# Second norm's rows turned by way of DRAM and VectorE, and the shared expert's gate and up weights held in TensorE while pairs of token tiles move

## The chip, the cores and the metric

The kernel runs on one core of a Trainium2 chip. The metric is device microseconds of that core for one execution, taken as the median of several executions.

## What is computed

1024 tokens (16 sequences of 64) of width 512 in float32 pass four residual blocks. The reference, cut to what matters here:

```
x = x + linear_attention(norm(x), ctx, ctx)
x = x + ffn(norm(x))                            # low rank, 1376 wide, gate and up with silu
x = x + cross_attention(norm(x), ctx)           # 16 heads of 96, 4 key/value heads; "second norm" here
x = x + moe(norm(x))                            # 16 experts, top 4, plus a shared expert

# cross attention: queries of the latents; keys and values of [context, latents]
hidden = concatenate([ctx, latents], axis=1)
q = latents @ Wq.T;  k = hidden @ Wk.T;  v = hidden @ Wv.T

# shared expert, 256 wide
out = out + silu(x @ Sg.T) * (x @ Su.T) @ Sd.T
```

The norms are numbered 1 (before the ffn), 2 (before the cross attention, the "second norm" of the title) and 3 (before the experts).

## The kernel before

Tokens are cut into J = 8 tiles of 128 rows; the width of 512 is KC = 4 chunks of 128. Every engine walks one hand-written list, `prog`, of steps such as ("ln_z", 2, j), and does its own part of each step in that order; semaphores tie the engines together. So the order of `prog` is the order in every engine's queue, and an instruction that waits holds up all behind it on its engine. SyncE (SP in the profile) has a straight list of transfers of its own, in which a wait holds up all later transfers too.

A matrix product wants the normalized rows turned, with the width on the partitions: the buffer zT. A norm of tile j is three steps. "ln_stat": VectorE takes mean and variance, GpSimd the root. "ln_z": VectorE writes the normalized rows to one of two row buffers, zrow (line 964). "ln_t": TensorE turns four blocks of 128x128 into a PSUM bank (line 1150, `transposes`), and ScalarE copies the bank to zT (line 631).

The places that the change touches, in order of time:

- The ffn runs over two halves of the tokens (h = 0, 1), each with NF = 11 slices c of the inner width. A step of the loop is f_gu(h, c), a gate and an up product of 512 columns (lines 1253 and 1254), a silu on ScalarE (689), a multiplication on VectorE (973), and f_z(h, c - 1), a product with the multiplied slice before (1263). The second norm of tiles 0 to 3 stands inside the loop of h = 1. Behind it are f_out of tiles 4 to 7 (TensorE line 1273, VectorE's addition line 979).
- Then come the queries of tiles 0 and 1, q(0, 0) to q(0, 3), and between them the key and value products of tiles 0 to 3; the second norm of tiles 4 to 7 stands there. VectorE and ScalarE copy each q out of PSUM (lines 986 and 699). The first scores, s(0), follow, and right behind them the first key product over tiles 4 to 7.
- The cross attention goes over 32 half sequences. Between its last steps stand the first sh_gu, the shared expert's gate and up products.
- In the tail, after the attention, stand the rest of the shared expert, the third norm of tile 7, its routing ("gate", "gate_v", "place", "count", "route") and "tables", a small product whose result tells every engine which rows and experts come when. Only then can SyncE load the first block of rows of the expert loop (line 411, four transfers of 64 KB that gather 32x128 pieces), VectorE turn it (line 891, 32x32 blocks) and TensorE begin with 36 blocks of the experts.

Shared expert, per tile j: sh_gu(j) multiplies the tile (stationary) with gate and up weights together (512 columns moving, four products); silu and multiplication give 256 columns zs, with the tokens on the partitions; sh_t(j) turns them on TensorE (two blocks), ScalarE copies them to zgT (line 753), and sh_d(j) multiplies with the down weights. The first four sh_gu are put aside (graw) and get their silu in the tail.

```
dense(ps[:, 4 + j % 2, :], lambda k: zT[:, k, j * P:(j + 1) * P],
      lambda k: wsh[:, k * D:(k + 1) * D], KC)
```

Of the kernel before, what the change touches and what calls it, by code (L numbers as in the profile page):

```python
# [12 lines left out]
P = 128  # L13
# [23 lines left out]
def build(nc, x_d, ctx_d, ctxT_d, cst_d, u1_d, v1_d, u2_d, v2_d, b1_d, b2_d,  # L37
# [3 lines left out]
    quads_d = slot_d.rearrange("(c a j) (b e) -> c b j a e", a=4, j=QD, b=4)  # L41

    id_d = nc.dram_tensor("slots", (P, 2 * P), F32, kind="Internal").ap()

    with ExitStack() as stack:
# [59 lines left out]
        zs = r1[:, 3072:3072 + J * I].rearrange("p (j i) -> p j i", j=J)  # L105
# [9 lines left out]
        kvm = sb("kvm", [P, 2, P])  # L115
        gw = sb("gw", [P, KC, E])
# [83 lines left out]
        s_z = sem("z_done")  # L200
        s_xb = sem("x1_plus_b2_done")
# [41 lines left out]
        s_ht = sem("shared_act_transposed")  # L243
        s_htc = sem("shared_act_copied")
# [80 lines left out]
        prog.append(("q", 0, 0))  # L325
        for i, u in enumerate(lat_units[0]):
# [5 lines left out]
            if 1 <= i < 5:  # L332
                prog.append(("ln_t", 2, 3 + i))
# [20 lines left out]
        for n in range(NU + 1):  # L354
# [22 lines left out]
            if n == 13:  # L377
# [3 lines left out]
        prog += [("sh_silu", j) for j in range(EARLY)]  # L381
        prog += [("op1", J - 1), ("ln_stat", 3, J - 1), ("place", J - 2), ("sh_t", 0), ("sh_gu", 4), ("ln_z", 3, J - 1),
                 ("sh_d", 0), ("ln_t", 3, J - 1), ("sh_t", 1), ("sh_d", 1), ("gate", J - 1), ("gate_v", J - 1), ("sh_gu", 5),
                 ("sh_t", 2), ("place", J - 1), ("count",), ("route", 0), ("sh_gu", 6), ("route", 1), ("sh_t", 3),
                 ("sh_d", 2), ("sh_d", 3), ("sh_gu", 7), ("tables",), ("sh_t", 4), ("sh_t", 5), ("sh_d", 4),
                 ("sh_t", 6), ("sh_d", 5), ("sh_t", 7), ("sh_d", 6), ("sh_d", 7)]

        def order(kinds):
            return {step: i for i, step in enumerate(p for p in prog if p[0] in kinds)}
# [26 lines left out]
        def kv_bank(n):  # L416

            return ps[:, 6 + n % 2 if n < EARLY_KV else 7, :]

# [5 lines left out]
        def _(sp):  # L425
# [40 lines left out]

            sp.wait_ge(s_fo, J)
# [3 lines left out]
            sp.dma_start(wv2, wv_d.rearrange("p (k m) -> p k m", k=KC)).then_inc(s_wkv2, 16)  # L471
            load_wo(0)
# [145 lines left out]
        def _(act):  # L618
# [15 lines left out]
            for step in prog:  # L634
# [109 lines left out]
                elif kind == "sh_silu":  # L744
                    j = step[1]
                    act.wait_ge(s_hraw, j + 1)
                    if j >= 2:
                        act.wait_ge(s_hz, j - 1)
# [379 lines left out]
        def _(pe):  # L1128
# [24 lines left out]
            def normed(layer, j):  # L1153

                pe.wait_ge(s_trc, TRN[("ln_t", layer, j)] + 1)
# [409 lines left out]
```

## Time and profile before

| | us |
|---|---|
| median of 3 runs | 711.25 |
| lowest and highest | 709.66, 711.31 |
| the profiled execution | 708.29 |
| its span, first to last instruction | 706.5 |
| TensorE busy | 682.1 (97%) |
| VectorE busy | 341.8 (48%) |
| ScalarE busy | 200.9 (28%) |
| mean granted TensorE clock | 0.994 |

The span is the stretch in which the profile sees instructions; the profiled execution's time holds 1.8 us more around it. Busy TensorE time is the union of its products' durations, of which each overlaps the next. In all rows a 32-bit product has two records, so that "x8" is four products; a turned block has one.

### The profile page before, as it was taken

The numbers are of one execution on the slowest core, as the hardware profiler recorded it, in microseconds if no ns is written. First come the engines' busy times: TensorE is split into PE (matmuls) and PEld (weight loads), VectorE is DVE, ScalarE is ACT, GpSimd is POOL, SyncE is SP. The second block draws the span as 40 slices with busy tenths as digits, with TensorE's granted clock in tenths as the row PEclk, the third lists the DMA queues.
The fourth block names the chain that finished last, engine by engine and source line by source line (L and its number), as shares of the span: only waits on it lengthen the run. The fifth ranks groups of instructions, "written<-read, shape, count | busy, mean of one in ns | idle before, by whom it ended". The sixth has DMA issues, their size and how long they took to land.

```text
span 706.5 us, 9696 instructions
## 1 busy us (share of the span) xinstructions
PE 682.1 (97%) x2444; PEld 394.6 (56%) x2445; DVE 341.8 (48%) x834; ACT 200.9 (28%) x563; POOL 176.2 (25%) x226
## 2 busy tenths in 40 slices
PE   9999899999999999999999999999999999999992
PEld 6555343446777777777776666554444444444440
DVE  4997433433224545686666667456233333333331
ACT  5453332313345433323333333231111111111110
POOL 2354210101000000004505233346023433333342
PEclk9999999999999999999999999999999999999997
DMA  9999997003000020001104003513866757768444
GB/s 341 409 421 420 422 420 320 1 29 150 1 1 0 1 90 0 1 1 61 60 1 150 30 31 111 189 60 92 274 164 111 179 103 186 183 131 234 92 73 60
DMA packets 54642, 98.99 MB, mean 140 GB/s; under 512 B 6560, under 2 KB 27808, under 8 KB 53952
## 3 DMA queue, kind: packets, MB, share of 16 engines
q1 hardware_dynamic: 24848, 69.41, 26.2%
q0 software_dynamic: 8816, 18.00, 12.7%
q10 hardware_dynamic: 20944, 11.15, 5.4%
q8 instruction: 18, 0.29, 0.2%
q14 instruction: 16, 0.13, 0.1%
HBM read 44.50 MB, written 54.17 MB: 140 GB/s over the span
## 4 chain that ended last, share of the span: by engine, by line
PE 81%; DMA 6%; DVE 5%; issue 2%; ACT 1%; POOL 1%; ACTq 1%; POOLq 1%; SPq 0%; DVEq 0%
PE ps L1159 46%; PE ps L1335 12%; DMA out<-rq,sidx 5%; PE ps L1304 4%; PE ps L1150 4%; PE ps L1320 4%; PE ps L1253 3%; PE ps L1254 3%; PE ps L1263 3%; DVE rq L941 2%; PE ps L1273 1%; DMA xr<-in_x 1%; DMA rq<-slot_rows 1%; DVE st L909 1%; ACTq L411 1%
## 5 line engine op out<-in xcount | busy, mean ns | idle before, releaser
L1159 PE MATMUL ps<-kv,rq 128*128 x432 | 192.4, 594 | 1.1 <-DVE rq L891 0.6
L1159 PEld LDWEIGHTS ps<-kv,rq 128*128 128x128 f32 x432 | 78.8, 190 | 88.3 <-issue 87.7
L1159 PE MATMUL ps<-zT,r 128*128 128x256 f32 (+1 forms) x424 | 103.4, 400 | 0.9 <-ACT kv L670 0.9
L1159 PEld LDWEIGHTS ps<-zT,r 128*128 128x128 f32 x424 | 79.4, 190 | 20.3 <-issue 10.2
L1335 PE MATMUL ps<-r 128*128 128x512 f32 x192 | 85.1, 593 | 0.0
L598 POOL DMA_INDIRECT out<-rq,sidx x36 | 56.7, 1574 | 110.7 <-DMA out<-rq,sidx 82.7
L525 POOL TENSOR_SCALAR ve<-mv 128x1 f32<-128x1 f32 x32 | 7.1, 223 | 292.4 <-DVE mv L910 292.4
L708 ACT ACTIVATE r<-ps,snm 128x128 f32<-128x128 f32 x128 | 45.3, 366 | 82.7 <-DVE snm L997 82.7
L1089 DVE TENSOR_TENSOR rq<-ps,rq 128x256 f32<-128x256 f32 x36 | 15.3, 424 | 97.3 <-ACT rq L764 97.3
L1335 PEld LDWEIGHTS ps<-r 128*128 128x128 f32 x192 | 35.2, 190 | 38.3 <-issue 38.3
L764 ACT ACTIVATE rq<-ps 128x256 f32<-128x256 f32 x36 | 13.8, 384 | 119.6 <-PE ps L1159 108.2
L986 DVE COPY rq<-ps 32x256 f32<-32x256 f32 x48 | 20.5, 427 | 50.8 <-PE ps L1159 50.3
L1100 DVE TENSOR_SCALAR rq<-ps,wts 128x512 f32<-128x512 f32 x36 | 27.0, 751 | 31.2 <-issue 13.3
L564 POOL DMA_INDIRECT slot_rows<-zrow,sloti x32 | 33.4, 1045 | 34.5 <-DVE sloti L1067 26.3
L1159 PE MATMUL ps<-r,zT 128*128 128x512 f32 (+1 forms) x96 | 39.9, 558 | 0.0
L1159 PE MATMUL ps<-r,rq 128*128 128x512 f32 x80 | 36.5, 595 | 1.0 <-ACT rq L753 1.0
L631 ACT COPY r<-ps 128x512 f32<-128x512 f32 x40 | 23.4, 586 | 45.8 <-PE ps L1150 45.7
L973 DVE SCALAR_TENSOR_TENSOR rq<-ps,r,rq 128x512 f32<-128x512 f32 (+1 forms) x22 | 16.4, 750 | 41.3 <-ACT rq L689 41.3
L1304 PE MATMUL ps<-kv,rq 96*128 96x128 f32 x256 | 34.8, 279 | 0.0
L1320 PE MATMUL ps<-r,kv 128*96 128x256 f32 x128 | 32.9, 379 | 1.3 <-DVE r L1013 1.3
L532 POOL DMA_INDIRECT slots<-tokw,sloti x32 | 31.2, 976 | 9.5 <-issue 9.5
L1304 PEld LDWEIGHTS ps<-kv,rq 96*128 96x128 f32 x256 | 32.6, 192 | 1.4
(176 smaller groups left out, 871.0 us busy)
## 6 DMA issues: line engine op xcount, KB each, us to landing
slot_rows<-rq SPq DMA_DIRECT2D x4, 8192.0 KB, 50.7
kv<-in_experts SPq DMA_DIRECT2D x54, 256.0 KB, 4.3
rq<-slot_rows ACTq DMA_DIRECT2D x136, 64.0 KB, 3.4
r<-in_Wq SPq DMA_DIRECT2D x1, 3072.0 KB, 21.3
r<-in_Wo SPq DMA_DIRECT2D x2, 1536.0 KB, 7.9
r<-in_ctx SPq DMA_DIRECT2D x8, 256.0 KB, 8.3
xr<-in_x SPq DMA_DIRECT2D x8, 256.0 KB, 8.4
out<-xr SPq DMA_DIRECT2D x8, 256.0 KB, 3.9
```

What stands on the lines that cost most here:

```text
L532: pool.indirect_dma_start(out=id_d.rearrange("a (b c) -> (a b) c", c=2), out_offset=bass.IndirectOffsetOnAxis(ap=sloti[:, j, k:k + 1], axi ...
L564: pool.indirect_dma_start(out=slot_d, out_offset=bass.IndirectOffsetOnAxis(ap=sloti[:, j, k:k + 1], axis=0), in_=zrow[:, LNN[("ln_z", 3, j ...
L598: pool.indirect_dma_start(out=out_d, in_=ylast[:, par, :] if last else yrow[:, par, :], in_offset=None, out_offset=bass.IndirectOffsetOnAx ...
L631: act.copy(dst, ps[:, n % 2, :] if len(dst.shape) == 2 else ps[:, n % 2, :].rearrange("p (k t) -> p k t", k=KC)).then_inc(s_trc, 1)
L708: e = act.activation(prob[:, n % 2, u, :], ps[:, 2 + n % 2, u * P:(u + 1) * P], ACT.Exp, bias=snm[:, n % 4, u:u + 1], scale=SCALE, accum_o ...
L1100: dve.tensor_scalar(ylast[:, par, :] if last else yrow[:, par, :], ps[:, 6 + par, :], wts[:, bass.ds(col, 1)], None, ALU.mult).then_inc(s_ ...
L1150: mm = pe.transpose(bank[:, c * P:(c + 1) * P], src[:, c * P:(c + 1) * P], ident)
L1159: mm = pe.matmul(out, lhs(k), rhs(k), start=(k == 0), stop=(k == n - 1))
L1253: pe.matmul(ps[0:m, 2 + n % 2, :], v1[:, c * P:c * P + m], pT, start=True, stop=True)
L1304: mm = pe.matmul(ps[:, 2 + n % 2, u * P:(u + 1) * P], qT[0:HD, q % 2, b % 4, h0:h0 + 2, :].rearrange("p h s -> p (h s)"), kT[0:HD, g, b, : ...
L1320: mm = pe.matmul(ps[0:HD, 6, 256 * g:256 * g + 256], v[:, b, c0:c0 + HD], probT[:, n % 2, 256 * g:256 * g + 256], start=True, stop=True)
L1335: mm = pe.matmul(ps[:, 7, :], oT[:, j % 2, m, :], wo[:, m, :], start=(m == 0), stop=(m == NQT - 1))
```

## The change

Two edits.

**The second norm's turning.** TensorE and ScalarE have no part in ("ln_t", 2, j) any more. SyncE stores the tile's 128x512 normalized rows to DRAM (256 KB), waits for that, and loads them again into a buffer zquad with four transfers of 64 KB, each of which gathers pieces of 128 floats for 32 partitions. VectorE turns zquad in blocks of 32x32 into zT. What lands in zT has the width in another order over partitions and chunks, and so have the weights Wq, Wk, Wv and the turned context, which the host lays out in that order; ScalarE writes the exponentials of the context in it as well. There is one zquad: the loads of tile j wait until tile j - 1 is turned. The steps of tiles 0 to 2 stand after slices 6, 8 and 10 of the ffn's second half, that of tile 3 behind its last f_out, those of tiles 4 to 7 one step later than before.

**The shared expert.** A sh_gu(i) now takes a pair of tiles: an even i gives the gates of pair i // 2, an odd one the ups. Blocks of 128 columns of the weights are stationary and 256 tokens move, eight products of 256 columns. The result has the inner width on the partitions, so sh_t, its turned blocks and ScalarE's copies, goes away; silu and multiplication are done once for a pair, over 512 columns.

```
     zrow_d = nc.dram_tensor("second_norm_rows", (2, P, D), F32, kind="Internal").ap()
     zquad_d = zrow_d.rearrange("n (a j) (b e) -> n b j a e", a=4, b=4)
...
-                if c % 2 == 0 and 1 <= i <= len(beside):
+                if h == 0 and c % 2 == 0 and 1 <= i <= len(beside):
                     prog.append(("ln_t", *beside[i - 1]))
+                if h == 1 and c in (6, 8, 10):
+                    prog.append(("ln_t", 2, c // 2 - 3))
...
-        prog.append(("q", 0, 0))
+        prog += [("ln_t", 2, 3), ("q", 0, 0)]
...
-            if 1 <= i < 5:
-                prog.append(("ln_t", 2, 3 + i))
+            if 2 <= i < 6:
+                prog.append(("ln_t", 2, 2 + i))
...
-        prog += [("sh_silu", j) for j in range(EARLY)]
-        prog += [("op1", J - 1), ("ln_stat", 3, J - 1), ("place", J - 2), ("sh_t", 0), ("sh_gu", 4), ("ln_z", 3, J - 1),
-                 ("sh_d", 0), ("ln_t", 3, J - 1), ("sh_t", 1), ("sh_d", 1), ("gate", J - 1), ("gate_v", J - 1), ("sh_gu", 5),
-                 ("sh_t", 2), ("place", J - 1), ("count",), ("route", 0), ("sh_gu", 6), ("route", 1), ("sh_t", 3),
-                 ("sh_d", 2), ("sh_d", 3), ("sh_gu", 7), ("tables",), ("sh_t", 4), ("sh_t", 5), ("sh_d", 4),
-                 ("sh_t", 6), ("sh_d", 5), ("sh_t", 7), ("sh_d", 6), ("sh_d", 7)]
+        prog += [("sh_silu", a) for a in range(EARLY // 2)]
+        prog += [("op1", J - 1), ("ln_stat", 3, J - 1), ("place", J - 2), ("sh_gu", 4), ("ln_z", 3, J - 1), ("sh_d", 0),
+                 ("ln_t", 3, J - 1), ("sh_d", 1), ("gate", J - 1), ("gate_v", J - 1), ("sh_gu", 5), ("place", J - 1),
+                 ("count",), ("route", 0), ("sh_gu", 6), ("route", 1), ("sh_d", 2), ("sh_d", 3), ("sh_gu", 7), ("tables",),
+                 ("sh_d", 4), ("sh_d", 5), ("sh_d", 6), ("sh_d", 7)]
...
+            def turn_rows(j):
+
+                sp.wait_ge(s_z, LNN[("ln_z", 2, j)] + 1)
+                sp.dma_start(zrow_d[j % 2], zrow[:, LNN[("ln_z", 2, j)] % 2, :]).then_inc(s_zst[j % 2], 16)
+                if j:
+                    sp.wait_ge(s_zt2, j)
+                sp.wait_ge(s_zst[j % 2], 16 * (j // 2 + 1))
+                for b in range(4):
+                    sp.dma_start(zquad[b * QD:(b + 1) * QD, :].rearrange("p (a e) -> p a e", a=4),
+                                 zquad_d[j % 2, b, :, :, :]).then_inc(s_zld, 16)
+
+            for j in range(4):
+                turn_rows(j)
             sp.wait_ge(s_fo, J)
             sp.wait_ge(s_xb, J)
             sp.wait_ge(s_act, 2 * NF)
             sp.dma_start(wk2, wk_d.rearrange("p (k m) -> p k m", k=KC)).then_inc(s_wkv2, 16)
             sp.dma_start(wv2, wv_d.rearrange("p (k m) -> p k m", k=KC)).then_inc(s_wkv2, 16)
+            for j in range(4, J):
+                turn_rows(j)
             load_wo(0)
...
+                        if old[1] == 2:
+                            dve.wait_ge(s_zst[old[2] % 2], 16 * (old[2] // 2 + 1))
...
+                elif kind == "ln_t" and step[1] == 2:
+                    j = step[2]
+                    dve.wait_ge(s_zld, 64 * (j + 1))
+                    dve.wait_ge(s_pt, j // 4 + 1)
+                    dve.transpose(zT[:, :, j * P:(j + 1) * P].rearrange("p k (a j) -> p a k j", a=4),
+                                  zquad[:, :].rearrange("p (a k i) -> p a k i", a=4, k=KC)).then_inc(s_zt2, 1)
...
                 elif kind == "sh_silu":
-                    j = step[1]
-                    act.wait_ge(s_hraw, j + 1)
-                    if j >= 2:
-                        act.wait_ge(s_hz, j - 1)
-                    act.activation(sg[:, j % 2, :], graw[:, j, 0:I], ACT.Silu).then_inc(s_hsil, 1)
-                elif kind == "sh_t":
-                    j = step[1]
-                    act.wait_ge(s_ht, j + 1)
-                    act.copy(zgT[:, j % 2, :], ps[:, 2 + j % 2, 0:I]).then_inc(s_htc, 1)
+                    a = step[1]
+                    act.wait_ge(s_hraw, 2 * a + 1)
+                    act.activation(shg[a], graw[:, 2 * a, :], ACT.Silu).then_inc(s_hsil, 1)
...
                 elif kind == "sh_gu":
-                    normed(3, j)
-                    dense(ps[:, 4 + j % 2, :], lambda k: zT[:, k, j * P:(j + 1) * P],
-                          lambda k: wsh[:, k * D:(k + 1) * D], KC).then_inc(s_hg, 1)
-                elif kind == "sh_t":
-                    transposes(ps[:, 2 + j % 2, :], zs[:, j, :], I // P).then_inc(s_ht, 1)
+                    normed(3, 2 * a)
+                    normed(3, 2 * a + 1)
+                    for c in range(2):
+                        at = (2 * hf + c) * P
+                        mm = dense(shared_bank(i)[:, c * 2 * P:(c + 1) * 2 * P], lambda k: wsh[:, k * D + at:k * D + at + P],
+                                   lambda k: zT[:, k, 2 * a * P:2 * (a + 1) * P], KC)
+                    mm.then_inc(s_hg, 1)
```

What it moves on VectorE, in the ffn's second half from its slice 6 to the first q: the rows "rq<-ps,r,rq" are the slices' multiplications, "zrow" the normalized rows, "xr<-ps,xr" the additions of f_out, "rq<-ps 32x4x64" the first q's copies. Before:

```order
L973 SCALAR_TENSOR_TENSOR rq<-ps,r,rq 128x512
L909 BN_STATS st<-xr 128x6
L910 BN_AGGR mv<-st 128x2
L973 SCALAR_TENSOR_TENSOR rq<-ps,r,rq 128x512
L964 TENSOR_SCALAR zrow<-xr,mv,rstd 128x512
L973 SCALAR_TENSOR_TENSOR rq<-ps,r,rq 128x512 x2
L973 SCALAR_TENSOR_TENSOR rq<-ps,r,rq 96x512
L979 TENSOR_TENSOR xr<-ps,xr 128x512 x4
L986 COPY rq<-ps 32x4x64 x3
```

The same place of the changed kernel, on VectorE, where lines 1005, 990, 1011 and 1018 are the former 973, 964, 979 and 986:

```order
L1005 SCALAR_TENSOR_TENSOR rq<-ps,r,rq 128x512
L932 BN_STATS st<-xr 128x6
L933 BN_AGGR mv<-st 128x2
L996 STREAM_TRANSPOSE zT<-zquad 128x4x4x32
L1005 SCALAR_TENSOR_TENSOR rq<-ps,r,rq 128x512
L990 TENSOR_SCALAR zrow<-xr,mv,rstd 128x512
L1005 SCALAR_TENSOR_TENSOR rq<-ps,r,rq 128x512
L996 STREAM_TRANSPOSE zT<-zquad 128x4x4x32
L1005 SCALAR_TENSOR_TENSOR rq<-ps,r,rq 128x512
L1005 SCALAR_TENSOR_TENSOR rq<-ps,r,rq 96x512
L996 STREAM_TRANSPOSE zT<-zquad 128x4x4x32
L1011 TENSOR_TENSOR xr<-ps,xr 128x512 x4
```

Four turnings have come in there (the fourth is the row behind the last one shown), each of which waits for its loads and stands ahead of a multiplication or an addition.

TensorE in the tail, from sh_t(0) to "count" before; "ps<-cst,r" are the blocks of sh_t, "r,zT" is sh_gu, "r,rq" sh_d, "cst,zrow" the third norm of tile 7, "gw,zT" its gate:

```order
L1150 MATMUL ps<-cst,r 128x128 x2
L1159 MATMUL ps<-r,zT 128x512 x4
L1159 MATMUL ps<-r,rq 128x512 x2
L1150 MATMUL ps<-cst,zrow 128x128 x4
L1150 MATMUL ps<-cst,r 128x128 x2
L1159 MATMUL ps<-r,rq 128x512 x2
L1159 MATMUL ps<-gw,zT 128x16 x4
L1159 MATMUL ps<-r,zT 128x512 x4
L1150 MATMUL ps<-cst,r 128x128 x2
L1352 MATMUL ps<-mask,cst 128x16
L1353 MATMUL ps<-mcum,cst 128x16
L1361 MATMUL ps<-mcum,cst 128x16
```

TensorE at the same place of the changed kernel; sh_d is now "ps<-r" and sh_gu "zT,r":

```order
L1196 MATMUL ps<-zT,r 128x256 x8
L1196 MATMUL ps<-r 128x512 x2
L1184 MATMUL ps<-cst,zrow 128x128 x4
L1196 MATMUL ps<-r 128x512 x2
L1196 MATMUL ps<-gw,zT 128x16 x4
L1196 MATMUL ps<-zT,r 128x256 x8
L1394 MATMUL ps<-mask,cst 128x16
L1395 MATMUL ps<-mcum,cst 128x16
L1403 MATMUL ps<-mcum,cst 128x16
```

The turned blocks are gone, and each sh_gu has become eight products of 256 columns instead of four of 512.

## Rows read from the trace of the kernel before

**Rows 1.** The page's first part: busy time, share of the span, instructions.
```profile
PE 682.1 (97%) x2444; PEld 394.6 (56%) x2445; DVE 341.8 (48%) x834; ACT 200.9 (28%) x563; POOL 176.2 (25%) x226
```

**Rows 2.** Timeline of TensorE, 143 to 200 us: start, duration, what, [idle before].
```profile
143.81 0.60 PE L1150 MATMUL ps<-cst,zrow 128*128 128x128 f32 x4
144.25 1.02 PE L1253 MATMUL ps<-rq,r 128*128 128x512 f32 x2
...
145.97 1.02 PE L1263 MATMUL ps<-rq,r 128*128 128x512 f32 x2
146.83 1.02 PE L1253 MATMUL ps<-rq,r 128*96 128x512 f32 x2
...
152.12 4.03 PE L1273 MATMUL ps<-r,rq 128*128 128x512 f32 x8 [0.68 <-ACT rq L693]
155.99 5.34 PE L1159 MATMUL ps<-zT,r 128*128 128x256 f32 x24
161.17 7.03 PE L1159 MATMUL ps<-zT,rq 128*128 128x512 f32 x16
168.03 0.60 PE L1150 MATMUL ps<-cst,zrow 128*128 128x128 f32 x4
...
199.09 1.06 PE L1304 MATMUL ps<-kv,rq 96*128 96x128 f32 x8
```

**Rows 3.** Timeline of VectorE, 124 to 166 us.
```profile
125.00 0.54 DVE L964 TENSOR_SCALAR zrow<-xr,mv,rstd 128x512 f32<-128x512 f32 x1
...
143.94 0.75 DVE L973 SCALAR_TENSOR_TENSOR rq<-ps,r,rq 128x512 f32<-128x512 f32 x1 [1.37 <-ACT rq L689]
...
153.36 0.69 DVE L979 TENSOR_TENSOR xr<-ps,xr 128x512 f32<-128x512 f32 x1 [3.09 <-PE ps L1273]
...
165.04 0.55 DVE L964 TENSOR_SCALAR zrow<-xr,mv,rstd 128x512 f32<-128x512 f32 x1 [1.42 <-POOL rstd L526]
```

**Rows 4.** VectorE's 32x32 turning, line 891: durations in ns, first and last start.
```profile
L891 DVE STREAM_TRANSPOSE rq<-rq x36: 699/701/712, 495.4 to 680.3; 128x512 f32<-128x512 f32 x36
```

**Rows 5.** Line 411's 64 KB loads: SyncE's eight in the timeline, and all 144.
```profile
488.38 4.41 SPq L411 DMA_DIRECT2D rq<-slot_rows  x8
...
DMA to landing us min/median/max: 1.8/3.4/7.7
```

**Rows 6.** Line 497's eight stores of 256 KB, each a tile's rows to DRAM.
```profile
DMA to landing us min/median/max: 2.9/3.9/4.3
```

**Rows 7.** Stretches: busy PE, PEld, DVE, ACT, POOL; clock; DMA share; GB/s.
```profile
127.00:150.00 23.00, 22.57 (x65) 10.43 (x63) 10.19 (x18) 7.97 (x13) 2.37 (x6) 1.00 0.00 1
488.00:497.00 9.00, 8.26 (x22) 3.75 (x23) 2.70 (x5) 1.13 (x4) 3.69 (x4) 1.00 0.56 157
```

**Rows 8.** Timeline of TensorE in the tail, 462 to 497 us.
```profile
462.47 0.42 PE L1150 MATMUL ps<-cst,r 128*128 128x128 f32 x2
462.73 3.60 PE L1159 MATMUL ps<-r,zT 128*128 128x512 f32 x8
...
468.32 0.38 PE L1150 MATMUL ps<-cst,r 128*128 128x128 f32 x2
469.43 1.98 PE L1159 MATMUL ps<-r,rq 128*128 128x512 f32 x4 [0.73 <-ACT rq L753]
...
476.16 0.38 PE L1361 MATMUL ps<-mcum,cst 128*128 128x16 f32 x2
...
487.08 0.25 PE L1386 MATMUL ps<-cst,cols 128*6 128x48 f32 x2
...
496.32 4.12 PE L1159 MATMUL ps<-kv,rq 128*128 x9 [0.58 <-DVE rq L891]
```

**Rows 9.** Timeline of VectorE in the tail: a shared multiplication, the routing's last row.
```profile
480.52 0.42 DVE L1077 TENSOR_TENSOR r<-ps,rq 128x256 f32<-128x256 f32 x1 [0.19 <-ACT rq L743]
...
485.71 0.17 DVE L838 TENSOR_REDUCE cols<-r 128x1 f32<-128x16 f32 x1
```

**Rows 10.** Chain of waits, the longest piece between "tables" and the expert loop.
```profile
489.91 5.42 DMA rq<-slot_rows
```

More of the change, by code:

```diff
@@ L115, in build @@
         kvm = sb("kvm", [P, 2, P])
+        zquad = sb("zquad", [P, D])
         gw = sb("gw", [P, KC, E])
@@ L200, in build @@
         s_z = sem("z_done")
+        s_zst = [sem(f"second_norm_stored{i}") for i in range(2)]
+        s_zld = sem("second_norm_loaded")
+        s_zt2 = sem("second_norm_transposed")
         s_xb = sem("x1_plus_b2_done")
@@ L656, in _ @@
                     copied(step, ekT[:, j % 2, :])
-                elif kind == "ln_t":
+                elif kind == "ln_t" and step[1] != 2:
                     copied(step, zT[:, :, step[2] * P:(step[2] + 1) * P])
@@ L959, in _ @@
                         old = [p for p in prog if p[0] == "ln_z"][n - 2]
-                        dve.wait_ge(s_tr, TRN[("ln_t", *old[1:])] + 1)
+                        if old[1] == 2:
+                            dve.wait_ge(s_zst[old[2] % 2], 16 * (old[2] // 2 + 1))
+                        else:
+                            dve.wait_ge(s_tr, TRN[("ln_t", *old[1:])] + 1)
                         if old[1] == 3:
@@ L1070, in _ @@
                 elif kind == "sh_silu":
-                    j = step[1]
-                    dve.wait_ge(s_hsil, j + 1)
-                    dve.tensor_tensor(zs[:, j, :], graw[:, j, I:2 * I], sg[:, j % 2, :], ALU.mult).then_inc(s_hz, 1)
-                elif kind == "sh_gu" and step[1] >= EARLY:
-                    j = step[1]
-                    dve.wait_ge(s_hsil, j + 1)
-                    dve.tensor_tensor(zs[:, j, :], ps[:, 4 + j % 2, I:2 * I], sg[:, j % 2, :],
-                                      ALU.mult).then_inc(s_hz, 1)
+                    a = step[1]
+                    dve.wait_ge(s_hsil, a + 1)
+                    dve.wait_ge(s_hraw, 2 * a + 2)
+                    dve.tensor_tensor(zs[:, a, :], graw[:, 2 * a + 1, :], shg[a], ALU.mult).then_inc(s_hz, 1)
+                elif kind == "sh_gu" and step[1] >= EARLY and step[1] % 2:
+                    i = step[1]
+                    a = i // 2
+                    dve.wait_ge(s_hsil, a + 1)
+                    dve.wait_ge(s_hg, i + 1)
+                    dve.tensor_tensor(zs[:, a, :], shared_bank(i), shg[a % 2], ALU.mult).then_inc(s_hz, 1)
                 elif kind == "sh_d":
@@ L1153, in normed @@
             def normed(layer, j):
-                pe.wait_ge(s_trc, TRN[("ln_t", layer, j)] + 1)
+                if layer == 2:
+                    pe.wait_ge(s_zt2, j + 1)
+                else:
+                    pe.wait_ge(s_trc, TRN[("ln_t", layer, j)] + 1)
             def dense(out, lhs, rhs, n):
@@ L1160, in dense, with shared_act @@
                 return mm
+            def shared_act(j, c):
+                at = (2 * c + j % 2) * P
+                return zs[:, j // 2, at:at + P]
             def half_unit(j, i):
@@ L1227, in _ @@
                               lambda k: weights[1][:, k, :], KC).then_inc(s_pr, 1)
-                elif kind == "ln_t":
+                elif kind == "ln_t" and step[1] != 2:
                     n = LNN[("ln_z", *step[1:])]
@@ L1388, in _ @@
                     j = step[1]
-                    pe.wait_ge(s_htc, j + 1)
+                    pe.wait_ge(s_hz, j // 2 + 1)
                     if j == 0:
```

60 lines of the change are left out of this document (31 added, 29 removed).

## The prediction

> **What bounds the kernel now.** I read the page first: TensorE is busy for 97% of the span [rows 1], so time on TensorE is the currency, and a change pays what it takes off TensorE, less what it makes TensorE wait. Then I read TensorE's timeline at the places of the two edits. Around the second norm, from 127 to 200 us, the reader is to see starts that follow each other without a gap: a slice of the ffn takes 146.83 - 144.25 = 2.58 us, and only around f_out is there a wait, 0.68 us [rows 2]. The tail is TensorE without idle time but for 0.73 us ahead of sh_d(1), up to "tables" at 487.08; behind it, the loop starts at 496.32, and what ends the wait for it is not the work that TensorE does in between but a transfer of the first rows, 5.42 us from issue to landing, and its turning [rows 8, 10].
>
> **First edit, what it takes off TensorE.** The four turned blocks of a tile start at 143.81, the next product at 144.25: 0.44 us a tile, eight tiles, **3.5 us** [rows 2]. All eight lie in the stretch without gaps. ScalarE's copies go too, and nobody waited for them. In the slices of the ffn that have no turned blocks beside them TensorE also runs at 2.58 us without a gap, so the loop is not held by silu and multiplication once the blocks are gone.
>
> **What it adds.** On VectorE a turning of 128x512, 0.70 us as in line 891 [rows 4]. On SyncE per tile a store of 256 KB, for which the nearest rows give 2.9 to 4.3 us to landing, median 3.9 [rows 6], and four loads of 64 KB, issued 4.41 / 8 = 0.55 us apart, each 1.8 to 7.7 us to landing, median 3.4 [rows 5]. I call the landing of a load L. Those rows come from stretches in which the DMA engines are busy for some 56% of the time; where tiles 0 to 3 are turned they are idle (share 0.00) [rows 7]. So I expect L near 1.8, take 3.4 as the careful value, and keep 7.7 as the far end.
>
> Whether this shows is a question of dates. I write what stands in the trace of before, less 0.44 us for each group of blocks already gone, and the store as 3.9.
>
> - Tile 0: its rows are ready at 125.5 [rows 3], loaded long before slice 6 is multiplied at 137.5 (slice 8's multiplication is at 143.94 before [rows 3], two slices and one group later than slice 6's, and two groups are gone by then). The turning waits in the queue behind that multiplication and the statistics of tile 3 (some 0.9 us) and ends at 139.8.
> - Tile 1: its loads wait for that; the last of four is issued at 141.55, and the turning ends at 141.55 + L + 0.7 = 145.7 with L = 3.4. The multiplication of slice 9, due at 145.2, moves back by 0.5 us. It has room: slice 8's ends at 144.69 and f_z wants it at 145.97 [rows 2, 3], 1.28 us later.
> - Tile 2: SyncE stores it once the loads of tile 1 are issued (142.1), the store lands at 146.0, the last load is issued at 147.7, the turning ends at 148.4 + L = 151.8. Behind it in the queue is the addition of f_out(4), due at 153.36 - 1.74 = 151.62 [rows 3], for which f_out(6) waits on TensorE: 0.2 us late at L = 3.4, nothing below 3.2.
> - Tile 3: stored at 148.3, landed 152.2, loads to 153.9, turned at 154.6 + L = 158.0. The key product that needs it is due at 161.17 - 1.74 = 159.43 [rows 2]; 1.4 us to spare. q(0, 0) needs only tiles 0 and 1.
> - Tiles 4 to 7: tile 4's rows are ready at 165.59 - 1.74 = 163.85 [rows 3]. A tile then takes store and four issues, 3.9 + 2.3 = 6.2 us, since the next store goes while the loads land. Tile 7 is stored at 182.5 and turned at 182.5 + 3.9 + 1.65 + L + 0.7 = 192.2. The product that needs it follows s(0), at 199.09 - 3.49 + 0.9 = 196.5 [rows 2]: 4.3 us to spare. VectorE's copies of q stand behind these turnings; q(0, 2) is the tight one: tile 6 is turned at 192.2 - 6.2 = 186.0, and q(0, 3), which wants the bank, starts 5.2 us ahead of s(0), at 190.4.
>
> Behind SyncE's waits stand Wk, Wv and Wo: Wk and Wv are issued at the old date, Wo once tile 7's loads are issued, before s(0), and its first use is well behind s(0). The first edit is thus worth 3.5 us, with 0 to 0.2 us back; I take 0. The ordered exponentials and the host's layouts change no count of bytes or columns; I cost them at nothing.
>
> The Trainium skill speaks against the edit: its page "VectorE: DVE Perf Modes", section "Rules for kernel authors", says to turn 128x128 on TensorE where PSUM will do as the destination, and on VectorE only blocks of 32. Turning by turning the rows agree (0.44 us on TensorE, 0.70 on VectorE, and a round trip besides). By that rule alone the edit loses; it is decided by who is idle, and that is the first rival below. "DMA: Bandwidth & Descriptors", section "Anatomy of one DMA", has some 2.0 us fixed plus bytes at 436 GB/s; by that, called an estimate, a load takes 2.2 us and a store 2.6, and no date above is missed.
>
> **Second edit.** Products: four of 512 columns cost (168.03 - 161.17) / 8 = 0.858 us each, eight of 256 cost (161.17 - 155.99) / 12 = 0.432 [rows 2], so a sh_gu costs 3.45 instead of 3.43, **0.2 us more** over eight. Taken away before "tables" are sh_t(0), 462.73 - 462.47 = 0.26; sh_t(1) with the wait behind it, 469.43 - 468.32 = 1.11 [rows 8]; sh_t(2) and sh_t(3), 0.22 each: **1.8 us**. sh_t(4) to (7) stand after "tables", where TensorE waits for rows anyway; they are worth nothing, and TensorE's idle time ahead of the loop grows from 0.58 to about 2 us. The multiplication and ScalarE's silu of a pair are wider but half as many; sh_d(0) finds zs(0) ready long before.
>
> Is "tables" still TensorE's to give? The routing on VectorE starts with "count" (476.16) and ends at 485.88, 9.7 us; TensorE comes to "tables" 10.9 us after "count" [rows 8, 9]. Afterwards 10.7 against some 9.3, since the 0.42 us multiplication inside the routing goes. TensorE stays later by 1.4 us. From "tables" on everything is a fixed lag (9.24 us to 496.32), so the loop starts 1.6 us plus 3.5 us earlier, and the loop itself is unchanged.
>
> **Sum.** 3.5 + 1.8 - 0.2 = 5.1 us off the profiled execution's 708.29, 703.2. The median of the runs shown is 2.96 us above that execution; the same 5.1 off 711.25 gives **706.1**.
>
> **Rivals.**
> 1. *The round trip is seen, and the kernel gets slower.* If loads land as slowly as the slowest of before, one buffer zquad makes a chain. Bound by landings, tile 1 ends at 142.25 + L, tile 2 at 144.7 + 2L, tile 3 at 147.15 + 3L against 159.43: a loss of 3L - 12.3, from L = 4.1. In the second four the loss is 4L - 19.1, from L = 4.8. Together 7L - 31.3: that eats the 5.1 us at L = 5.2 and is 2.1 us slower than before from L = 5.5; at 7.7 it is 22.6 lost, a time of 728.8. For it: a load of this very shape took 5.42 us at 489.91. Against it: there the engines were busy for 56%, here for nothing. Chance 0.05. A partial form, L from 3.6 to 4.8, costs 0.5 to 3 us and gives 706.6 to 709; 0.10.
> 2. *The tail gives nothing.* The landing of the first rows is set by other traffic (GpSimd's scatters), not by "tables"; then a start of 1.6 us less is eaten and 3.5 us remain: 707.8. For it: 5.42 against a median of 3.4. Against it: those scatters come from the same chain, which moves as well. 0.12.
> 3. *The change does less than it says*, because VectorE's queue holds back the multiplications of the ffn or the copies of q by more than their room: 1 to 3 us lost somewhere, 707 to 709; in 0.08 I put all such. Anything that gives more than 5.5 us, such as shorter waits at the loop's start, 0.05.
>
> **Chances.** The forecast holds with 0.60 and has 705.3 to 707. A change of under 0.3% (2.1 us) cannot be told from none here. Faster by more: all of the forecast, the second rival, and most of the others, 0.87; within: 0.07; slower: 0.06. For eight in ten I go from 703.5 (the runs' own spread and some more gain) to 709.
>
> **What would show it.** Right: no rows "ps<-cst,zrow" between 127 and 185, slices of 2.58 us, q(0, 0) at about 154.2, s(0) at 195.6, "tables" at 482.0, the loop at 491.2. Right for the round trip: landings below 3 us and VectorE's turnings with no waits by TensorE behind them. Wrong: an idle gap of TensorE at f_out(6), ahead of the first key product or behind s(0), released by a turning; or "tables" early while the first transfer's landing grows by as much. A clock below 1.00 after the 2 us gap ahead of the loop would also break the sum.

## The result

The changed kernel took 708.55 us (median of 20 runs, 707.03 to 713.04), the kernel before 711.7 us on the same chip (20 runs, 709.66 to 714.65): a ratio of 0.996, 95% interval 0.9947 to 0.9974. It is faster by 3.15 us; 5.1 were forecast. Executions of one kernel spread over some 5 us on this chip, so the medians of 20 are compared. The profiled execution of the changed kernel took 709.7 us, with a span of 707.6 and a mean granted clock of 0.987.

The page's first part, answering to [rows 1]:

```profile
PE 679.5 (96%) x2460; PEld 404.0 (57%) x2461; DVE 346.2 (49%) x838; ACT 193.3 (27%) x543; POOL 176.3 (25%) x226
```

TensorE's timeline at the first edit, answering to [rows 2]:

```profile
149.19 1.12 PE L1305 MATMUL ps<-rq,r 96*128 96x512 f32 x2 [0.76 <-DVE rq L1005]
150.99 4.03 PE L1315 MATMUL ps<-r,rq 128*128 128x512 f32 x8 [0.68 <-ACT rq L720]
154.85 5.34 PE L1196 MATMUL ps<-zT,r 128*128 128x256 f32 x24
160.03 10.46 PE L1196 MATMUL ps<-zT,rq 128*128 128x512 f32 x24
...
196.19 1.06 PE L1346 MATMUL ps<-kv,rq 96*128 96x128 f32 x8
```

The turned blocks are gone, TensorE waits for no turning, and s(0) starts 2.90 us earlier, though this execution's first transposition came 0.77 us later (9.27 against 8.50). The new transfers in the page's part on DMA issues (count, KB each, median us to landing):

```profile
second_norm_rows<-zrow SPq DMA_DIRECT2D x8, 256.0 KB, 2.2
```

And the four loads a tile, from the view of the buffer zquad (least, median and most of their time to landing):

```profile
DMA to landing us min/median/max: 1.8/1.9/2.3
```

The tail of TensorE, answering to [rows 8]:

```profile
482.80 0.25 PE L1425 MATMUL ps<-cst,cols 128*6 128x48 f32 x2 [0.21 <-issue]
483.50 7.10 PE L1196 MATMUL ps<-r 128*128 128x512 f32 x16 [0.44 <-issue]
496.01 10.08 PE L1196 MATMUL ps<-kv,rq 128*128 x16 [5.41 <-SPq L520]
```

"tables" is 4.28 us earlier than before, but the loop starts only 0.31 us earlier: 13.21 us lie between them instead of 9.24, TensorE is idle for 5.41 of these, and the loop's first row (sixteen records, eight products) then takes 10.08 us (7.13 in an execution without this, below). The 0.21 us ahead of "tables" is a wait for the routing, whose last row on VectorE ends at 482.75 here. What the other engines did behind "tables", from the timelines of ScalarE, VectorE and SyncE:

```profile
486.11 0.19 ACT L779 CAST tab<-ps 6x48 int32<-6x48 f32 x1 [9.77 <-remote]
...
482.67 1.28 DVE L1119 TENSOR_TENSOR xr<-ps,xr 128x512 f32<-128x512 f32 x2
484.06 0.69 DVE L1112 TENSOR_TENSOR r<-ps,rq 128x512 f32<-128x512 f32 x1
492.44 1.29 DVE L1119 TENSOR_TENSOR xr<-ps,xr 128x512 f32<-128x512 f32 x2 [7.68 <-remote]
...
488.87 6.89 SPq L418 DMA_DIRECT2D rq<-slot_rows  x8
```

ScalarE takes the tables' product 3.3 us after it started, where 0.3 to 0.4 is usual. VectorE adds sh_d(4) at 492.44, though the product was done before 486. SyncE issues the first load 6.07 us after "tables" (1.30 before) and needs 6.89 us for the eight (4.41 before, [rows 5]). This slowness of all three is called the lateness below. The stretches of the windows view (answering to [rows 7]; the number behind POOL's is the granted clock) show no traffic to blame, with a DMA share of 0.30 where before had 0.56, and the clock:

```profile
488.00:497.00 9.00, 3.59 (x8) 1.31 (x7) 2.58 (x4) 0.00 (x0) 2.52 (x3) 0.90 0.30 73
497.00:515.00 18.00, 18.00 (x44) 8.12 (x43) 4.64 (x8) 2.48 (x8) 0.18 (x1) 0.86 0.79 263
```

The two mean clocks together stand for (0.10 x 9 + 0.14 x 18) / 0.5 = 6.8 us at 1.2 GHz, at the end of the idle time and behind it.

The lateness is not only behind "tables". A shared multiplication on VectorE, some 9 us ahead of "tables", comes 2.04 us later than in the undisturbed execution of the same program (the second row, from the first group below), and the whole routing with it:

```profile
473.75 0.69 DVE L1112 TENSOR_TENSOR r<-ps,rq 128x512 f32<-128x512 f32 x1 [2.59 <-remote]
```

```profile
471.71 0.69 DVE L1112 TENSOR_TENSOR r<-ps,rq 128x512 f32<-128x512 f32 x1 [0.55 <-PE ps L1196]
```

### The profile page after: what moved, and what is told of

Read it like the earlier page. It is cut to its first block, busy times and chain, and to the rows that moved or that the text cites. A ratio compares the mean times of both kernels' runs of the same rounds, so it can differ in the third digit from the quotient of the medians.

```text
span 707.6 us, 9751 instructions
## 1 busy us (share of the span) xinstructions
PE 679.5 (96%) x2460; PEld 404.0 (57%) x2461; DVE 346.2 (49%) x838; ACT 193.3 (27%) x543; POOL 176.3 (25%) x226
## 4 chain that ended last, share of the span: by engine, by line
PE 79%; issue 8%; DVE 4%; DMA 3%; SPq 2%; ACT 1%; POOL 1%; POOLq 0%; DVEq 0%; ACTq 0%
PE ps L1196 48%; PE ps L1377 9%; PE ps L1346 4%; PE ps L1184 4%; PE ps L1362 4%; PE ps L1295 3%; PE ps L1296 3%; PE ps L1305 3%; DVE rq L964 2%; DMA r<-in_ctx 2%; DMA out<-rq,sidx 1%; PE ps L1315 1%; SPq L412 1%; SPq L418 1%; PE ps L1237 1%
## 5 line engine op out<-in xcount | busy, mean ns | idle before, releaser
L1196 PE MATMUL ps<-kv,rq 128*128 x432 | 195.3, 601 | 6.0 <-SPq L520 5.4
L1196 PE MATMUL ps<-zT,r 128*128 128x256 f32 (+1 forms) x552 | 132.5, 395 | 0.9 <-ACT kv L697 0.9
L1196 PEld LDWEIGHTS ps<-zT,r 128*128 128x128 f32 x552 | 103.4, 190 | 24.5 <-issue 11.2
L964 DVE RECIPROCAL rq<-ps 128x512 f32<-128x512 f32 x8 | 26.8, 3354 | 5.5 <-PE ps L1238 5.5
L1043 DVE COPY r<-ps 96x192 f32<-96x192 f32 x64 | 19.8, 348 | 19.1 <-PE ps L1362 18.5
```

Of the source, the lines that this page charges most:

```text
L964: link(dve.reciprocal(srec, ps[:, 5, :]))
L1196: mm = pe.matmul(out, lhs(k), rhs(k), start=(k == 0), stop=(k == n - 1))
```

## The experiments

All kernels of one group ran on one chip, beside runs of the kernel before on that chip; the three groups were on three chips. The theory after the first result: the change gives what it should up to "tables"; what is lost is the lateness and the low clock behind it. The rival: the tail gives nothing by the way the change is built. "Late" and "undisturbed" are said of a kernel's one profiled execution; the median is of all its runs.

**First group** (before: 709.19 us, 17 runs).

*First edit alone*: norm 2's rows through DRAM, the shared expert as before.

> The first edit alone (second norm turned by way of DRAM and VectorE; shared expert as before). Theory A, the loss sits in the tail: in the changed kernel's profile the first edit already showed its whole 3.5 us (s(0) 2.9 us earlier with a start 0.6 us later), so alone it gives 3.5 us off, ratio about 0.995, TensorE's granted clock stays at 1.00 up to the end of the loop (mean 0.994), and the gap ahead of the expert loop stays below 1.5 us. Rival B, the first edit costs something elsewhere (extra waits in the loop, or the longer program): ratio 0.997 or more, mean clock below 0.992.

Measured: 704.25 us (6 runs), ratio 0.9931 (0.9916 to 0.9945), a gain of 4.9 us: theory A, with 1.4 us more than its 3.5. The profile is undisturbed.

*Second edit alone*: the pairs, with norm 2 turned on TensorE.

> The second edit alone (shared expert's pairs; second norm as before). Theory A, what the second edit saves before the tables it gives back at the start of the expert loop: TensorE now idles there for more than 2 us, its granted clock falls to 0.5 for some 7 us, and the first products of the loop take some 3 us more; ratio 1.000 to 1.002, mean clock 0.987 to 0.990. Rival B, the idle gap costs nothing and the edit gives its 1.6 us: ratio 0.998, mean clock 0.994.

Measured: 707.2 us, ratio 0.9964 (0.9947 to 0.9982), its 12 runs spread from 703.59 to 709.45: neither theory, 2.0 us faster than before. Its profile is that of the slowest run. Nothing is late up to the loop, but VectorE then waits 5.09 us for a transfer of rows, TensorE is idle for 3.02 us inside the loop's start, and half clock follows.

*The changed kernel with fillers* that nothing reads:

```
 last_down()
+for n in range(5):
+    pe.matmul(ps[:, 5, :], ident, wsh[:, 0:D], start=True, stop=True)
```

> The changed kernel with five products of 512 columns put behind sh_d(7), ahead of the first gate and up product of the loop; their result is overwritten and nobody reads it. Theory A: TensorE idles some 4.3 us less there, its clock stays at 1.00 and the loop's first 16 records take 7.1 us instead of 10.1; ratio to the kernel before 0.992 to 0.994, mean clock 0.994. Rival B, the lower clock is not due to the gap, or costs nothing: ratio 0.996 as for the changed kernel, or above it where the rows come before the five products are through.

Measured: 705.79 us (6 runs), ratio 0.9952 (0.9935 to 0.997). No lateness and no gap here, so it does not decide between the theories.

*The changed kernel itself again.*

> The changed kernel once more, to see on the same chip how far its tail repeats. Theory A: ratio 0.996, mean clock 0.987 to 0.990, TensorE idle for 2 us or more ahead of the loop and at clock 0.5 in its first products. Of the profiled execution's late rows (the tables copied 3.3 us after their product, SyncE's four loads issued 1.4 us apart in place of 0.5): if they are a property of the kernel they are there again, if they belong to that execution the gap is about 2 us.

Measured: 701.65 us (701.26 to 702.01, 4 runs), ratio 0.9892 (0.9873 to 0.9911). Here the lateness was absent. Its tail, TensorE and then SyncE:

```profile
482.51 0.25 PE L1425 MATMUL ps<-cst,cols 128*6 128x48 f32 x2
482.69 7.13 PE L1196 MATMUL ps<-r 128*128 128x512 f32 x16
490.34 7.13 PE L1196 MATMUL ps<-kv,rq 128*128 x16 [0.52 <-DVE rq L914]
...
483.73 4.43 SPq L418 DMA_DIRECT2D rq<-slot_rows  x8
```

The same program, with "tables" at the same place within 0.3 us, starts the loop 5.7 us earlier than in the first profile and is 6.9 us faster in the median, on a chip where before is 2.5 us faster. The fillers, useless where nothing is late, held the loop back to 493.53 and cost 4.1 us.

**Second group** (before: 711.14 us, 31 runs): is the lateness the rule, what does an idle gap cost, and how much room has the round trip?

*The changed kernel a third time.*

> The changed kernel itself once more, beside the others of this call. In its first 20 runs it took 708.55 us, in the first experiment's company 701.65 (before: 709.19), and the difference stands in the trace at the expert loop's start: engines that take 2 to 7 us longer to react, 5.41 us of idle TensorE, then half clock. Theory A (that lateness is not a part of the change, but comes with some loadings of a program): the loop starts at about 490.3 and the time is 701 to 702.5 where it is absent, 706 to 709 with a granted clock below 0.990 where it is there; nothing in between stands on the tables or the turned rows. Theory B (the change's own shorter tail makes the lateness, and the 701.65 was luck): 707 to 709 here again.

Measured: 709.57 us (708.51 to 711.19, 10 runs), ratio 0.9978 (0.996 to 0.9995). The time is above both theories' ranges by some 0.5 us and does not part them; the lateness is back, in the same shape:

```profile
483.99 0.25 PE L1425 MATMUL ps<-cst,cols 128*6 128x48 f32 x2 [0.20 <-issue]
484.68 7.11 PE L1196 MATMUL ps<-r 128*128 128x512 f32 x16 [0.44 <-DVE xr L1119]
496.86 9.99 PE L1196 MATMUL ps<-kv,rq 128*128 x16 [5.08 <-DVE rq L914]
...
487.91 8.54 SPq L418 DMA_DIRECT2D rq<-slot_rows  x8
```

*Two dummy loads ahead of the first rows*:

```
+for r in range(2):
+    sp.dma_start(zquad[0:QD, :]..., zquad_d[0, 0, :, :, :]).then_inc(s_ex, 16)
+    sp.wait_ge(s_ex, 16 * (r + 1))
 for i in range(2):
     block_of = sp.value_load(tab[0:1, i:i + 1], min_val=0, max_val=P)
```

> The changed kernel with two dummy loads of 64 KB, one after the other, in SyncE's queue ahead of the first rows' loads: some 4 to 6 us more of idle TensorE ahead of the loop, as in the changed kernel's first profile but made on purpose. Theory A (an idle gap of this length costs more than itself, since the clock falls to half behind it; in the first profile 6.8 us at half clock cost 3 us): the granted clock is 0.5 for some microseconds behind the gap, and the time is the gap plus about 3 us above the changed kernel of this call, 708 to 711. Theory B (the gap costs itself alone, and the half clock had another cause): clock 1.00 and 705.5 to 707.5.

Measured: 711.84 us (10 runs), ratio 1.0004 (0.9985 to 1.0022): 2.3 us over the changed kernel of this group. The gap is there, 7.60 us of idle TensorE ahead of a loop at 497.80, and half clock behind it. But the changed kernel already had 5.08 us of gap and half clock on this chip, so the two loads added 2.5 us of gap, and these cost 2.3 us: of the price of half clock this comparison says nothing.

*The same with seven fillers.*

> The same two dummy loads, with seven products of 128x512 that nothing reads behind the last product of the shared expert (some 6.2 us of TensorE in the gap). Theory A: the clock stays at 1.00 and it is about 3 us faster than the one without the fillers, though it does more. Theory B: no faster than that, and slower by up to 1 us where the fillers outlast the landing.

Measured: 711.38 us (10 runs), ratio 0.9991 (0.9975 to 1.0008). The loop's first products (timeline) and a stretch from there on (windows), of the kernel without fillers and then of the one with them:

```profile
497.80 8.80 PE L1201 MATMUL ps<-kv,rq 128*128 x16 [7.60 <-SPq L525]
```

```profile
498.00:515.00 17.00, 17.00 (x42) 7.78 (x43) 4.66 (x9) 2.48 (x8) 0.00 (x0) 0.91 0.87 285
```

```profile
493.07 6.17 PE L1484 MATMUL ps<-r,cst 128*128 128x512 f32 x14
501.13 7.13 PE L1201 MATMUL ps<-kv,rq 128*128 x16 [1.89 <-SPq L525]
```

```profile
501.00:515.00 14.00, 13.27 (x35) 6.22 (x36) 4.26 (x8) 1.68 (x5) 0.00 (x0) 1.00 0.87 284
```

That a long gap of TensorE is followed by half clock, and that products in the gap prevent it, is shown: theory A had the mechanism. Its price of 3 us is not borne out. The loop's first row took 1.7 us more (8.80 against 7.13), and yet from the loop's start to the end of the span both need the same (708.0 - 497.80 = 210.2; 711.2 - 501.13 = 210.1). The medians differ by 0.5 us, which these runs cannot tell from nothing, and not by 3. Over all fourteen profiles the same stretch takes 208.1 to 210.2 us where the loop starts at full clock and 210.2 to 214.0 us where half clock stands at its start (214.0 is the second edit alone in the first group, with its 3.02 us of gap inside the stretch). So any price from nothing to some 3 us fits, and it was not measured alone.

*Each tile's store three times in series* (round trip 4.4 us longer):

```
+for r in range(2):
+    sp.dma_start(zrow_d[j % 2], zrow[...]).then_inc(s_ex, 16)
+    sp.wait_ge(s_ex, 16 * (2 * j + r + 1))
 sp.dma_start(zrow_d[j % 2], zrow[...]).then_inc(s_zst[j % 2], 16)
```

> The changed kernel with every tile's store made three times, each waiting for the one before (a store lands in 2.2 us, so each round trip is 4.4 us longer). Theory A (the round trip is hidden by dates: tile 2's turning has 2 us of room ahead of the addition of f_out(4), tile 3's 3 us, tile 7's 9 us): by the dates of the profile tile 2 is now turned at 154.0 and holds f_out(6) back by about 1.8 us, tile 3 costs 0.5 more, tile 7 is turned at 200 where it is wanted at 197 to 199; 4 to 7 us slower than the changed kernel of this call. Theory B (the engines that wait for it have slack behind these dates): less than 2 us slower.

Measured: 712.8 us (10 runs), ratio 1.0024 (1.001 to 1.0039), 3.2 us over the changed kernel of this group. VectorE's turnings of tiles 2, 3 and 7, and TensorE where it waits:

```profile
151.09 0.71 DVE L1000 STREAM_TRANSPOSE zT<-zquad 128x512 f32<-128x512 f32 x1 [2.42 <-DMA zquad<-second_norm_rows]
159.71 0.71 DVE L1000 STREAM_TRANSPOSE zT<-zquad 128x512 f32<-128x512 f32 x1 [2.98 <-DMA zquad<-second_norm_rows]
...
199.41 0.71 DVE L1000 STREAM_TRANSPOSE zT<-zquad 128x512 f32<-128x512 f32 x1 [6.04 <-DMA zquad<-second_norm_rows]
```

```profile
193.47 5.42 PE L1200 MATMUL ps<-zT,r 128*128 128x256 f32 x24 [1.39 <-issue]
198.73 1.06 PE L1350 MATMUL ps<-kv,rq 96*128 96x128 f32 x8
200.38 8.85 PE L1200 MATMUL ps<-zT,r 128*128 128x512 f32 x32 [0.59 <-DVE zT L1000]
```

The first four tiles still hide all of it, since tile 2 is turned at 151.8 (154.0 by my dates, which put its store too late); the last ones show 1.39 + 0.59 = 2.0 us. (VectorE's copies of a q, at 192.11 behind tile 6's turning at 191.47, free the bank that the first of these waits for.) So a round trip 4.4 us longer a tile costs a few microseconds and no more: between the two theories.

**Third group** (before: 713.07 us, 21 runs): which edit brings the lateness?

*First edit alone, again.*

> The first edit alone once more, to see on a chip where the changed kernel's engines react late what each edit does there. Theory A (the lateness comes with the second edit's products, twice as many instructions on TensorE in the tail): tables to loop takes 8.5 to 9.2 us with ScalarE's CAST of the tables 0.4 us behind them, no half clock at the loop, 4 to 5 us faster than before (ratio about 0.994). Theory B (the lateness has nothing to do with either edit and comes with the chip): the CAST comes 1.5 to 3.5 us late here too and the ratio is above 0.996.

Measured: 706.97 us (706.2 to 707.37, 4 runs), ratio 0.9907 (0.9881 to 0.9933). TensorE, VectorE and SyncE in the tail:

```profile
484.01 0.25 PE L1423 MATMUL ps<-cst,cols 128*6 128x48 f32 x2
...
492.70 3.72 PE L1196 MATMUL ps<-r,rq 128*128 128x512 f32 x8 [2.75 <-ACT rq L778]
496.26 7.03 PE L1196 MATMUL ps<-kv,rq 128*128 x16
...
492.23 1.29 DVE L1119 TENSOR_TENSOR xr<-ps,xr 128x512 f32<-128x512 f32 x2 [7.27 <-remote]
...
486.55 8.14 SPq L420 DMA_DIRECT2D rq<-slot_rows  x8
```

Neither theory: the lateness is here too (VectorE 7.27 us, SyncE 8.14 for eight issues), but it sets in later, after the CAST, which comes 0.4 us behind "tables". TensorE's idle time comes in pieces between turned blocks, the longest 2.75 us, and its clock stays at 1.00.

*Second edit alone, again.*

> The second edit alone. Theory A: the late reactions are here (ScalarE's CAST 1.5 us or more behind tables, idle TensorE of 3 us or more at the loop's start, granted clock below 0.990) and eat the 1.6 to 3 us that it saves: ratio 0.998 to 1.003. Theory B: as in the first experiment's company, ratio 0.996.

Measured: 712.33 us (10 runs), ratio 0.9984 (0.9966 to 1.0002). "tables" at 486.28, the loop at 499.14 behind 5.06 us of idle TensorE, mean clock 0.986 to 0.990 over its runs: theory A.

*First edit, and the old gate and up products in halves*:

```
-dense(ps[:, 4 + j % 2, :], lambda k: zT[:, k, j * P:(j + 1) * P],
-      lambda k: wsh[:, k * D:(k + 1) * D], KC).then_inc(s_hg, 1)
+for hf in range(2):
+    mm = dense(ps[:, 4 + j % 2, hf * I:(hf + 1) * I], lambda k: zT[:, k, j * P:(j + 1) * P],
+               lambda k: wsh[:, k * D + hf * I:k * D + (hf + 1) * I], KC)
+mm.then_inc(s_hg, 1)
```

> The first edit alone, with each sh_gu(j) of the old shared expert done as eight products of 256 columns instead of four of 512: the second edit's count of TensorE instructions (64 instead of 32 a pair of tiles) without its pairs and without its order. Theory A (the instruction count makes the lateness): late reactions appear, TensorE idles ahead of the loop, 3 to 6 us slower than the first edit alone. Theory B (it is the order or the removed steps that matter): 0.2 us of product time more and no lateness, same as the first edit alone within 1 us.

Measured: 714.46 us (10 runs), ratio 1.0014 (0.9993 to 1.0034): 7.5 us slower than the first edit alone, for 0.2 us of product time, so theory A, by more than it said. TensorE and ScalarE in the timeline:

```profile
485.44 0.25 PE L1425 MATMUL ps<-cst,cols 128*6 128x48 f32 x2
485.62 0.66 PE L1184 MATMUL ps<-cst,r 128*128 128x128 f32 x4
494.25 3.78 PE L1196 MATMUL ps<-r,rq 128*128 128x512 f32 x4 [7.98 <-ACT rq L778]
...
504.09 7.03 PE L1196 MATMUL ps<-kv,rq 128*128 x16
...
488.89 0.38 ACT L768 ACTIVATE rq<-ps 128x256 f32<-128x256 f32 x1 [9.81 <-remote]
491.02 0.19 ACT L781 CAST tab<-ps 6x48 int32<-6x48 f32 x1 [1.75 <-remote]
```

No other kernel reacts so late: the silu of sh_gu(7) 3.4 us behind its product (485.4), the CAST 5.6 us behind "tables". The products are the same work on the same tiles; their number is doubled and their width halved, and with the number that of the loads of stationary blocks. Not all of the 7.5 us is lateness: the two profiles differ by 9.3 us, of which 6.4 lie between "tables" and loop (18.65 against 12.25) and 1.3 stand already at s(0), ahead of every product that the edit changes, where this execution had half clock at f_out (5.48 us for 4.03).

*The changed kernel with ScalarE kept busy*:

```
+elif kind == "sh_d" and step[1] < J - 1:
+    act.wait_ge(s_hd, step[1] + 1)
+    act.copy(spare[:, 16 * step[1]:16 * step[1] + 16], ident[:, 0:16])
```

> The changed kernel with seven tiny copies of 16 columns on ScalarE, one behind each product of sh_d, which nothing reads; ScalarE, idle for 9.8 us ahead of the tables' CAST in the changed kernel, then works at the same places as sh_t's copies did before. Theory C (an engine that has waited for long reacts late): the CAST comes 0.3 us behind tables, the loads are issued 2 to 3 us earlier, and it is 3 to 5 us faster than the changed kernel, ratio about 0.992. Theory A or B: the same as the changed kernel, 0.996 to 0.998.

Measured: 709.86 us (6 runs), ratio 0.9942 (0.9921 to 0.9964). The CAST still comes 2.6 us behind "tables" (485.16, 482.55), and "tables" to loop takes 12.95 us as in the kernel without the copies (12.87 in the second group). Theory C falls; that the ratio is nearer to 0.992 than to 0.998 is not explained by it, and the changed kernel itself did not run on this chip.

## Why the prediction was right, and where it was not

**First edit, 3.5 us: right.** Two profiles differ at s(0) by this edit alone and start alike (the first transposition at 9.24 and 9.27): the second edit alone has s(0) at 199.68, the changed kernel at 196.19, 3.49 us. Forecast dates of q(0, 0) and s(0) were 154.2 and 195.6, measured 154.85 and 196.19, both some 0.6 us later, in an execution whose start was 0.77 us late. L was 1.9 us, as hoped from the idle engines, and the store took 2.2 us, not the 3.9 that I wrote for it from [rows 6]; all dates of the chain had more room than I gave them. Rival 1 is excluded by landings of at most 2.3 us, and with trip times 4.4 us longer it would have cost 3.2 us. The Trainium skill's rule for VectorE ("VectorE: DVE Perf Modes", "Rules for kernel authors") is right turning by turning (0.70 us against 0.44) and did not decide, since TensorE was the engine without idle time. The Trainium skill's formula ("DMA: Bandwidth & Descriptors", "Anatomy of one DMA") gave an estimate of 2.2 and 2.6 us for load and store, and the trace has 1.9 and 2.2; the section fits it to DMAs that GpSimd issues, where SyncE issued these. By the medians the first edit alone gained more than 3.5 us, 4.9 and 6.1 on two chips. Of the surplus the undisturbed profile shows 0.75 us between "tables" and loop (8.49 against 9.24) and 1.3 behind it (208.8 against 210.2), which the prediction had put at nothing.

**Second edit ahead of "tables", 1.6 us: right where nothing is late.** From s(0) to "tables" it was 287.99 us before and is 286.33 in the changed kernel's undisturbed profile and in the second edit alone: 1.66. In the result's profile it is 286.61. The 1.4 us by which TensorE was to come later than the routing were gone there, since the routing had slipped by 2.04 us and ended 0.05 us ahead of "tables".

**"From tables on everything is a fixed lag (9.24 us)": this step failed**, and with it "the loop itself is unchanged" and TensorE's idle time of "about 2 us". The runs showed two lags in its place:

| profile | "tables" to loop, us | longest idle, us | half clock at the loop |
|---|---|---|---|
| before | 9.24 | 0.58 | no |
| changed, first group | 7.83 | 0.52 | no |
| first edit alone, first / third group | 8.49 / 12.25 | 0.24 / 2.75 | no / no |
| second edit alone, first / third group | 7.67 / 12.86 | 3.02 / 5.06 | yes / yes |
| changed, the result / second group | 13.21 / 12.87 | 5.41 / 5.08 | yes / yes |

(The 3.02 us lie inside the loop's start, behind its second block's products.) Without the lateness the tail gives more than forecast, because the first rows' transfers end earlier after "tables" (the last of the four took 4.08 us against 5.42 before): the lag shrinks by 1.4 us, the loop to the end by 0.9, and the changed kernel won 7.5 us. With it, the changed kernel loses 5.0 to 5.4 us between "tables" and loop (13.21 and 12.87 against 7.83), and in the result's profile 2.3 more behind it, where the low clock stands: from the loop's start to the span's end it is 211.6 us there, 209.3 in the undisturbed one. How much of the 2.3 is the clock's is not shown, as the pair with and without fillers says. I had named a clock below 1.00 behind the gap as what would break the sum, and it came, behind a gap of 5.4 us, not of 2. The gain in the medians, 3.15 us, is 4.4 less than the undisturbed 7.5, and the time lands 2.4 us above the forecast value, 0.45 of them because before itself stood at 711.7 and not at 711.25. Two errors of opposite sign, a lag that can shrink and a lateness that eats it, kept it in the range: that part is luck. By time it lies nearest to rival 2 (707.8), "the tail gives nothing", and by place too, but its mechanism is not that one: GpSimd's scatters kept their pace of 1.27 us each, and the DMA share was lower than before.

**What the lateness is: part shown, part open.** Shown: it holds TensorE's tail up in kernels with either edit, it is absent on one of three chips where several programs ran (there only the second edit alone had a 3.0 us gap, for another reason), and doubling the number of TensorE's products at equal work makes it worse: 6.4 us more between "tables" and loop, in one profile each on one chip. The second edit doubles them as well: a pair of tiles needs sixteen products of 256 columns where it needed eight of 512. That this is why the changed kernel suffers more than the first edit alone is argued from that comparison; it was not tried inside the pairs, for instance with four tiles and 512 columns moving. Open is what is slow underneath. The late engines are marked "remote", and SyncE's own register moves stretch to 0.7 us with no wait in them, so no single wait explains it, as the chain of the changed kernel's first profile shows (start, length, engine's queue, line):

```profile
487.47 0.69 SPq L418
488.17 0.70 issue
488.87 0.01 SPq L418
488.88 0.68 issue
489.56 0.70 SPq L418
```

A transfer of instructions is not seen there either: the trace has none between 476 and 508 us.

One regularity stands in every late profile, and no run tested it: the lateness ends just behind GpSimd's scatters, the indirect stores of rows and slots for the experts. In the result's profile the last scatter ahead of the loop is

```profile
489.44 0.96 POOL L558 DMA_INDIRECT slots<-tokw,sloti  x1 [0.30 <-issue]
```

and ends at 490.40; SyncE is back to its pace at 492.40, VectorE works again at 492.44. In all nine late profiles the last wait of VectorE or ScalarE that is marked "remote" ends 2.0 to 2.2 us behind that point. The earlier piece of lateness ends the same way, in the seven late profiles that hold the pairs: VectorE and ScalarE move 1.4 to 1.6 us behind the end of the row of eight scatters before. The scatters run at the same pace in the undisturbed profiles, so they are not enough by themselves; whether the lateness goes with them is an open rival to the count of products, and moving or thinning them is the experiment that is missing. The profile of before shown here is one without the lateness, at 708.29 us, 3.4 below the median of its chip. Whether its other runs have it, the profiles at hand don't tell, but their mean clocks hint at it: on the third group's chip only the fastest of 21 (709.75 us) has 0.994, fifteen have 0.990 or less, and the slowest (716.14) has 0.987, while the first edit alone keeps 0.993 to 0.994 there. So the changed kernel's gain in the medians cannot be split exactly: its own loss by the profiles, 7.7 us, is more than the 4.4 that the medians miss.

**The version that beat before most evenly** is the first edit alone: ratios 0.9931 and 0.9907 on two chips, where the changed kernel had 0.996, 0.9892 and 0.9978 on three. On the one chip where both ran the changed kernel was 2.6 us faster; on the third it was not run.

## What to carry to other kernels

A turning moved off the engine without idle time paid its busy time there (3.49 us for 3.5), since the round trip's last date was earlier than its reader's; write these dates down, and for transfers in an idle stretch try the shortest landing seen beside the median of a busy one (1.8 and 3.4 us here, 1.9 measured). A lag behind a small product that passes through three other engines is not a constant: work that TensorE has left covers it, and a shorter tail can turn into idle time. Try wide products before narrow ones of the same column time: halving the width and doubling the number cost up to 7.5 us in this kernel, on the one chip where it ran, where the columns said 0.2.

## What the hardware did that I had not expected

- VectorE, ScalarE and SyncE can react 2 to 8 us late for a stretch of 10 us, with little DMA traffic (a share of 0.30 from 488 to 497 us in the result's profile, 0.56 in before) and TensorE's array running on. The same program took 701.65 us on one chip and 709.57 on another, where before differed by 2 us; whether the chip or the program's loading decides was not told apart.
- Half clock appeared at a second place in four of eleven profiles of kernels that hold the first edit, at f_out, where TensorE's gaps are only 0.76 and 0.68 us long: the four products there (eight records) took 5.4 to 5.5 us instead of 4.03. In the second group's changed kernel:

```profile
150.71 5.50 PE L1315 MATMUL ps<-r,rq 128*128 128x512 f32 x8 [0.68 <-ACT rq L720]
```

```profile
148.00:160.00 12.00, 10.56 (x30) 5.87 (x30) 4.75 (x7) 0.66 (x2) 0.00 (x0) 0.86 0.28 91
```

The gaps are as long in profiles that keep the full clock, and why it falls in some was not found. Both gaps stand in the kernel before as well. The four are, in the second group, the changed kernel, the one with loads and fillers and the one with three stores, and in the third the one with halved products; where one of these is set against a profile without it, some 1.3 us of the difference can be this.
